# Four sums in DRAM instead of two for the routed experts of a decoder, with four result tiles and four reads at the end

## The reference

```python
logits = jnp.einsum('th,eh->te', x, gate_w)             # 64 experts
scores = softmax(logits)
topk_w, topk_ids = jax.lax.top_k(scores, 6)
topk_w = topk_w / (jnp.sum(topk_w, axis=-1, keepdims=True) + EPS)
comb = zeros((T, 64)).at[arange(T)[:, None], topk_ids].add(topk_w)
g, u = split(einsum('th,efh->tef', x, w_gate_up))       # 176 each
act = silu(g) * u * comb[:, :, None]
routed = einsum('tef,ehf->th', act, w_down)
shared = silu(x @ ws_gate.T) * (x @ ws_up.T) @ ws_down.T
x = layernorm(x + routed + shared)
```

## Time and profile before

| | |
|---|---|
| median of 3 runs | 3301.8 us (3299.2 to 3311.94) |
| the profiled execution, its span from the first to the last instruction | 3378.8 us, clock of TensorE 0.853 in the mean |
| TensorE busy | 2632.3 us (78%) |
| VectorE busy | 1810.1 us (54%) |
| ScalarE busy | 1526.6 us (45%) |
| GpSimd busy | 1228.9 us (36%) |
| DMA over the span | 192.73 MB, 57 GB/s in the mean |

### The profile page before, as it was taken

How to read it: one execution, slowest core, us unless ns; L and a number is a source line. 1 busy time by engine, 2 the same in 40 slices (tenths; PEclk the granted TensorE clock), 3 DMA queues, 4 the chain that set the end, 5 groups by cost and what they waited for, 6 DMA issues and landing times. The chain is left out here.

```text
span 3378.8 us, 47321 instructions
## 1 busy us (share of the span) xinstructions
PE 2632.3 (78%) x13662; PEld 1672.9 (50%) x13663; DVE 1810.1 (54%) x3839; ACT 1526.6 (45%) x2976; POOL 1228.9 (36%) x1164
## 2 busy tenths in 40 slices
PE   5799999888999994777759558885578335988984
PEld 2467777655777773444435323332445112555652
DVE  4666676585666665888851367773222501222334
ACT  3555555464555550888951136663255100223321
POOL 1477777536777771000000100000000172244443
PEclk8999999999999996666659769997689656899997
DMA  2121121003112101900000000000000051477875
GB/s 63 47 57 26 56 57 33 13 7 88 34 49 57 38 13 62 340 1 1 1 30 0 17 1 1 1 1 4 18 1 0 26 181 49 93 165 171 179 172 125
DMA packets 127073, 192.73 MB, mean 57 GB/s; under 512 B 17552, under 2 KB 88208, under 8 KB 125584
## 3 DMA queue, kind: packets, MB, share of 16 engines
q1 hardware_dynamic: 83696, 134.71, 14.1%
q0 software_dynamic: 23616, 33.24, 5.6%
q10 hardware_dynamic: 19584, 22.57, 2.4%
HBM read 123.23 MB, written 67.25 MB: 56 GB/s over the span
## 5 line engine op out<-in xcount | busy, mean ns | idle before, releaser
L228 DVE SCALAR_TENSOR_TENSOR h_pre<-h_px,h_par,h_pre 128x510 f32<-128x510 f32 (+2 forms) x384 | 286.4, 746 | 268.7 <-ACT h_pre L689 248.9
L652 PE MATMUL h_po<-h_wo,h_h 128*128 128x256 f32 x1024 | 328.2, 411 | 0.0
L2890 POOL DMA_INDIRECT moe_sums<-ex_y,ex_sidx x132 | 204.9, 1553 | 314.9 <-DVE ex_y L3058 296.7
L574 POOL TENSOR_SCALAR h_decay<-h_cumb,h_sel 128x256 f32<-128x256 f32 x256 | 292.4, 1142 | 25.2 <-DMA h_cumb<-cum_rows 25.2
L585 POOL TENSOR_TENSOR h_mix<-h_decay,cb 128x768 f32<-128x768 f32 x128 | 232.6, 1817 | 164.3 <-ACT h_decay L675 164.3
L616 PE MATMUL h_px<-x_cols,h_w 128*128 128x512 f32 x512 | 254.4, 620 | 25.3 <-DMA h_d<-d_skip 25.3
L843 POOL TENSOR_TENSOR norm_rstd<-norm_mv,mhalf 128x4 f32<-128x4 f32 x24 | 28.3, 1178 | 605.0 <-DVE norm_mv L826 605.0
L621 PE MATMUL h_pz<-x_cols,h_w 128*128 128x512 f32 x512 | 242.8, 597 | 5.6 <-DVE h_gate L742 5.6
L701 ACT ACTIVATE h_xt<-h_pxt,h_sel 128x128 f32<-128x128 f32 x512 | 146.0, 368 | 152.1 <-PE h_pxt L640 152.1
L2935 PE MATMUL ex_pg<-ex_w,ex_xT 128*128 x528 | 196.1, 495 | 21.8 <-ACT ex_xT L2993 6.2
L654 PEld LDWEIGHTS h_pss<-ones,h_sq 128*128 128x128 f32 x1024 | 194.6, 190 | 26.3
(11 more groups left out here) (389 smaller groups left out, 5823.6 us busy)
## 6 DMA issues: line engine op xcount, KB each, us to landing
h_cumb<-cum_rows SPq DMA_DIRECT2D x32, 1024.0 KB, 8.5
moe_tiles<-blank SPq DMA_DIRECT2D x4, 6642.0 KB, 44.2
ex_w<-moe_w SPq DMA_DIRECT2D x64, 352.0 KB
ex_xg<-moe_tiles ACTq DMA_DIRECT2D x136, 162.0 KB
ex_wd<-moe_wd SPq DMA_DIRECT2D x64, 176.0 KB
h_w<-w_xg SPq DMA_DIRECT2D x8, 1024.0 KB, 10.4
moe_sums<-blank SPq DMA_DIRECT2D x2, 2176.0 KB, 26.7
h_wo<-w_out SPq DMA_DIRECT2D x8, 512.0 KB, 10.2
```

The source lines that it names most:

```text
L228: ins = dve.scalar_tensor_tensor(out=out[:, :, back:S], in0=src[:, :, 0:S - back], scalar=par[:, at + CK - 1 - back:at + CK - back], in1=o ...
L574: pool.tensor_scalar(decay[j][:, u, 0:S], cumb[s.vb][:, j, u, :], sel[s.vb][:, u * TPB, 1, j:j + 1], 0.0, ALU.subtract, ALU.min)
L652: pe.matmul(po[t // TPB][:, t % TPB, :], hh[j % 2][:, t * P:(t + 1) * P], w_out[s.pg][:, j, :], start=(j == 0 and t % TPB == 0), stop=(j = ...
L2890: pool.indirect_dma_start(out=r.sums[i % 2][:, :], out_offset=bass.IndirectOffsetOnAxis(ap=sidx[i][:, 0:1], axis=0), in_=y[i % 2][:], in_o ...
```

## The change

There are four sums, one for each tile of the ring, with a semaphore each; four result tiles `y[i]` and four `back[i]`. GpSimd's wait at L2888 is for the scatter of tile j-4 into the same of the sums, and isn't there in the first round. VectorE's wait in `note` names the semaphore of the slot. The two waits ahead of the last two tiles are gone. SP blanks four sums, reads four back, and VectorE adds four.

```diff
-        self.sums = [nc.dram_tensor(f"moe_sums{i}", (T + P, E), F32, kind="Internal").ap() for i in range(2)]
+        self.sums = [nc.dram_tensor(f"moe_sums{i}", (T + P, E), F32, kind="Internal").ap() for i in range(RING)]
...
-        y = [sb(f"y{i}", [P, E]) for i in range(2)]
-        back = [sb(f"back{i}", [P, NT, E]) for i in range(2)]
+        y = [sb(f"y{i}", [P, E]) for i in range(RING)]
+        back = [sb(f"back{i}", [P, NT, E]) for i in range(RING)]
...
-        summed = [sem(f"summed{i}") for i in range(2)]
+        summed = [sem(f"summed{i}") for i in range(RING)]
...
-            for i in range(2):
-                sp.wait_ge(summed[i], (more + 1) * (PER * 16))
+            for i in range(RING):
+                sp.wait_ge(summed[i], (more + 1) * 16)
                 sp.dma_start(back[i][:], r.sums[i][0:T, :].rearrange("(n p) e -> p n e", p=P)).then_inc(finished, 16)
...
-            pool.wait_ge(r.blanked, 6 * 16)
+            pool.wait_ge(r.blanked, (4 + RING) * 16)
...
-                if not isinstance(g, int) or i >= 2:
-                    pool.wait_ge(summed[i % 2], (g * PER + i // 2) * 16)
+                if not isinstance(g, int):
+                    pool.wait_ge(summed[i], g * 16)
                 pool.sem_inc(released)
-                pool.indirect_dma_start(out=r.sums[i % 2][:, :], out_offset=bass.IndirectOffsetOnAxis(ap=sidx[i][:, 0:1], axis=0),
-                                        in_=y[i % 2][:], in_offset=None, compute_op=ALU.add).then_inc(summed[i % 2], 16)
+                pool.indirect_dma_start(out=r.sums[i][:, :], out_offset=bass.IndirectOffsetOnAxis(ap=sidx[i][:, 0:1], axis=0),
+                                        in_=y[i][:], in_offset=None, compute_op=ALU.add).then_inc(summed[i], 16)
...
                 if past is not None:
-                    dve.wait_ge(summed[i % 2], (past * PER + i // 2 + 1) * 16)
+                    dve.wait_ge(summed[i], (past + 1) * 16)
...
-                dve.tensor_scalar(y[n][:], po[n][:, 0:E], wt[i][:, 0:1], None, ALU.mult).then_inc(weighed, 1)
+                dve.tensor_scalar(y[i][:], po[n][:, 0:E], wt[i][:, 0:1], None, ALU.mult).then_inc(weighed, 1)
...
-            dve.wait_ge(summed[0], (more * PER + 1) * 16)
             weigh(more * RING + RING - 2, 0, 2)
-            dve.wait_ge(summed[1], (more * PER + 1) * 16)
             weigh(more * RING + RING - 1, 1, 3)
-            dve.wait_ge(finished, 32)
+            dve.wait_ge(finished, RING * 16)
             dve.drain()
-            for i in range(2):
+            for i in range(RING):
                 dve.tensor_tensor(r.x[:], r.x[:], back[i][:], ALU.add)
                 dve.drain()
```

More of the change, by code:

```diff
@@ L2827, in experts_stage @@
         NC = T // C
-        PER = RING // 2
         TURNS = TILES // RING
```

## The result

The changed kernel takes 3325.15 us (median of 8 runs, 3319.04 to 3332.04), the kernel before, in 8 runs, 3308.26 (3299.2 to 3315.44). The ratio of the runs is 1.0048, 95% interval 1.0031 to 1.0064: 16 us slower, at the very edge of the 0.5% that I had called visible. By the medians it is 16.9 us. The forecast was 3317, or +15.5.

What follows compares the result with a forecast made beforehand. The prediction took the loop to be bound by the ring note, `ex_y`, scatter, landing, note, with TensorE close behind. Its terms, +7.5 +9.0 -0.7 -0.3 +0 = +15.5 us, on 3301.8 gave 3317 us, range 3303 to 3332.

Steps and rivals of the forecast that it cites:

- The loop, 0: Loop over the experts' tiles: no gain, since VectorE's note still waits for the scatter of tile j-4; 0 us.
- The ring: Loop: note, `ex_y`, scatter, landing, next note follow each other and bound the loop, 6.49 us for two tiles.
- The reads, +7.5: End of the kernel: two more reads of sums, 6.0 us each with the DMA engines full; +7.5 us.
- The adds, +9.0: After the reads: two more adds on VectorE with nothing beside them, drains included; +9.0 us.
- The removed waits, -0.3: Last two tiles: two waits fall away, so the last `ex_y` starts sooner after its matmul; -0.3 us.
- GpSimd's arithmetic, -0.7: GpSimd at L2888: the value to wait for is computed once per round instead of twice; -0.7 us.
- The blanks, 0: First cross attention: two more blanks keep SP some 28 us longer, covered by its 313.6 us of waiting; 0 us.
- the forecast's own case: Whole kernel: the ring stays and the tail grows; +15.5 us, own range +7.5 to +18.7, chance 0.60.
- The second: Loop: it opens up, GpSimd runs ahead with four scatters and TensorE becomes the bound; -34 us, 3268, chance 0.05.
- The third: End of the kernel: the reads are hidden and only the last one counts; +8 us, 3310, chance 0.15.
- The fourth: Loop: scatter landings get longer, from twice the memory or meeting the reads; +13 us, 3330, chance 0.14.
- the fifth: Loop: scatter landings get shorter; -13 us, 3304, chance 0.06.

Runs made afterwards that it cites:

- The loop alone: The changed kernel with only two of its four sums read back and added, half of the experts' tiles left out; 3312.92 us, ratio 1.0015.
- note last: The changed kernel with VectorE's note moved behind hide and weigh: 3325.86 us; the same order with two sums and four result tiles: 3309.68 us.
- late numbers: The changed kernel with note's wait moved to the copy into sidx, ahead of `ex_y`: 3298.34 us; with two sums and four result tiles 3284.28.
- the adds one by one: Four sums, note's wait moved to the copy into sidx, each add waiting only for its own read: 3286.81 us; with two sums 3278.22.
- the blanks alone: The kernel before with four sums blanked but two used, GpSimd waiting for all the blanks; 3311.36 us, ratio 1.0006.

## Why the prediction was right

**The loop, 0.** Right: 269.7 us of VectorE's wait and 3.27 us a tile. It is shown from both sides. The loop alone gains nothing, and the place of VectorE's wait, which the change left, gives 27 us when it is moved with four sums; with two it gives 16, or 22 together with four result tiles. The ring that I had read from two turns holds in the mean of the whole loop too: worked out from all rows of L3048, L3058 and L2890 in the first profile, 0.67 us lie between note and `ex_y`, 1.34 between `ex_y` and its scatter, 4.48 between the scatter and the note that waits for it, 6.49 together. The reason given, that GpSimd's wait was over before `weighed` came, is confirmed by the kernels in which it need not be, those with two sums, four result tiles and VectorE's wait out of the way: only there is GpSimd put down as waiting on the DMA (31.2 us with note last, 27.2 and 27.9 with late numbers). The first note and the last are 428.9 us apart in the changed kernel and 420.6 to 430.7 in the four profiles with the old loop, so that a cost of a few us is not excluded.

**The reads, +7.5.** From the last note to the first add there are 3284.71 - 3254.05 = 30.7 us; in the two profiles before 23.4 (3352.55 - 3329.2) and 23.8 (3271.81 - 3248.0). That is +7.1 with the 0.3 for the removed waits in it, where I had 7.2. I had 28.1 us from the first issue to the first add (3360.1 - 3332.0), and it is 28.3. That the rate of the full engines sets it, 349 GB/s then and 352 now, is borne out by the adds one by one, which followed the reads 6.0 to 6.6 us apart. The fit of the Trainium skill (DMA: Bandwidth & Descriptors, Anatomy of one DMA) that I had held against it is the page's for DMAs that GpSimd issues, and these reads are issued by SP: it should not have been called the price of them. Its 436 GB/s are not reached in any of these stretches.

**The adds, +9.0.** 17.93 us against 8.93.

**The removed waits, -0.3.** Not seen. The last `ex_y` waits for TensorE now (2.79 us), whose last down product took 2.07 us: the granted clock was 0.53 in the mean between 3258 and 3262 us, for the most part its lower level (0.50, 1.2 GHz), where the same product ran in 1.13 us at 1.00 in the first profile before. This is not the change's doing. In the second profile of the kernel before, with both waits still in place, that product took 2.07 us as well, and its `ex_y` waited for it; with the blanks alone it took 1.12, and its `ex_y` began 0.39 us after its end, held by the DMA as in the earlier trace rows. TensorE's idle time just ahead of the product doesn't tell the two cases apart: 1.40 and 1.20 us where it took 1.13 and 1.12, 1.21 and 0.44 us where it took 2.07. The term was read from one profile, and whether the waits were worth 0.3 us is not settled.

**GpSimd's arithmetic, -0.7.** The computation was halved as I said, but 35 ns in each of 32 rounds is far below what profiles of one loop differ by (10 us). Not settled.

**The blanks, 0.** Right, by the kernel with them alone (1.0006) and by the unchanged 369.8 us; SP's 28 us more were 12.5: one blank kept SP for 20.1 us before and after the change, so that the 28.30 of the earlier trace rows were no price for two more. The cover of 313.6 hid it either way.

**The sum** was 15.5 and the ratio gives 15.9 (0.0048 x 3308.3), the medians 16.9. That the two agree to an us or so is in part luck: the interval of the ratio reaches from +10 to +21, and the two small savings in the sum were not seen. The time itself, 3325 against 3317, is off by 8, and 6.5 of it are the base: I started from the median of three runs, 3301.8, and eight gave 3308.3. So the time lies above the 3309 to 3321 that I had given the forecast's own case, while the difference lies inside its +7.5 to +18.7. By the ratio, just under 0.5%, the outcome is what I had called no change (0.54).

**The rivals.** The second, the loop opens, didn't happen in this change. Its bound, TensorE's 49.7 us of idle time, is not reached in the experiments either: the best loops take 398.5 to 401 us from the first note to the last, 20 to 26 under the two profiles of the old one (420.6 and 424.8). The third, the reads are hidden, is ruled out by the 30.7 us from the last note to the first add. The Trainium skill's hint at repeating gaps (Perfetto Trace Analysis, Optimization Strategy) speaks of the engine that should be saturated, here TensorE, while the 269.1 us of gaps that I had set against it are VectorE's. It holds for this loop in part: deeper result tiles are worth 8 us, but only once VectorE's own wait is out of the way; deeper sums are worth nothing. The fourth and the fifth, longer or shorter landings, are not seen beyond the spread of the profiles: from a scatter to the note that waits for it there are 4.53 and 4.58 us in the mean with four sums (the changed kernel, the loop alone) and 4.40 to 4.53 in the four profiles with the old loop.

**A number of the experiments.** The one for the late note was wrong because I followed the moved wait and not the moved `noted`, which ScalarE waits for.

## What to carry to other kernels

Before doubling a buffer, follow the order of the engine that releases the waiter: the wait to be weakened may be implied by an older one, further up in another engine's program. The table of waits says so by whom it names: here GpSimd was waiting on VectorE, never on the DMA, and VectorE was waiting for the DMA because of a tile of 128 numbers. Move such a wait to just ahead of the instruction that overwrites what is still being read, and check who waits for whatever is moved with it. And sums that are kept apart are paid for at the end, with a read and an add each. The adds can run beside the reads, but even so four sums cost 9 us more than two here (3286.81 against 3278.22).

## What the runs showed of the hardware that I had not expected

In the first profile of the kernel before, eight of the adds of the shared experts (L3040) came 10 to 12 us apart and the stretch to the first note was 77 us longer than in the second profile. The line in the first:

```profile
L3040 DVE TENSOR_TENSOR x_rows<-ex_po,x_rows x32: 415/425/426, 2727.4 to 2903.1; 128x256 f32 x32
...
  remote: 53.2, 5
  PE ex_po L2916: 30.2, 20
```

And in the second:

```profile
L3040 DVE TENSOR_TENSOR x_rows<-ex_po,x_rows x32: 414/425/426, 2715.2 to 2810.7; 128x256 f32 x32
...
  PE ex_po L2916: 40.0, 24
```

The starts reach from 2727 to 2903 us in the one, from 2715 to 2811 in the other. The instructions are the same and as long as ever (425 ns); between them VectorE stood idle for 10 to 11.5 us each time and TensorE for most of it, while GpSimd went on with its scatters of the tokens' rows at the usual pace (963 ns each, 960 in the second profile). None of the twelve later profiles (the changed kernel and the eleven experiments) has such gaps. The cause is open, and no experiment was made on it; it only says that a span 2.3% over the median of the runs should be looked into before two traces are held against each other stage by stage.
